# Moving Pool's power and ratio, the swap matmul and DVE's reciprocal within one round of an eight-batch language-model tower

## The reference

```python
h = tok(x)                                # embedding, causal 2-tap conv, relu
h = h + attn(layernorm(h), ...)           # linear recurrence, kept in logs, 4 heads x 64 states
#   x = exp(log_x - max over the 64 states + 2);  y = x @ C + u @ D
h = h + ffn(layernorm(h), ...)
#   normed -> x_attn = normed @ attn_w.T + attn_b + x
#   h1 = gelu(x_attn @ fc1.T + b1); y = h1 @ fc2.T + b2; out = gelu(y @ next_w.T + next_b)
```

## Time and profile before

| what | us |
|---|---|
| median of 3 runs | 189.66 (189.43 to 189.98) |
| the profiled execution, its own time | 189.79 |
| its span in the trace | 188.0 |
| PE busy, share of the span | 168.9, 90% |
| PE weight loads | 153.9, 82% |
| DVE busy | 136.7, 73% |
| POOL busy | 111.0, 59% |
| ACT busy | 107.4, 57% |

### The profile page before, as it was taken

One profiled execution on the slowest core, in us unless ns is written; L12 is line 12 of the kernel. 1 busy time (PEld: TensorE's weight loads), 2 busy tenths in 40 slices (PEclk: granted clock), 3 DMA queues, 4 the chain that ended last, 5 costly groups with the idle time before them and its releaser, 6 DMA issues.

```text
span 188.0 us, 3890 instructions
## 1 busy us (share of the span) xinstructions
PE 168.9 (90%) x1327; PEld 153.9 (82%) x1327; DVE 136.7 (73%) x409; ACT 107.4 (57%) x285; POOL 111.0 (59%) x178
## 2 busy tenths in 40 slices
PE   0497899999999998899898899999999999988972
PEld 0196779999999997787687799999998999987961
DVE  1859975765534546658988999998888896647993
ACT  3027997645543235434455484967949596775661
POOL 3106764799800000324979596696978969697761
PEclk9999999999999999999999999999999999999999
DMA  5994000000000000000000000000010100101103
GB/s 144 335 432 171 5 0 5 2 0 0 3 0 0 3 0 0 2 3 0 0 0 3 0 2 0 3 24 33 0 59 0 59 0 20 39 3 58 56 0 112
DMA packets 2327, 7.42 MB, mean 39 GB/s; under 512 B 254, under 2 KB 892, under 8 KB 2052
## 3 DMA queue, kind: packets, MB, share of 16 engines
q1 hardware_dynamic: 2162, 7.05, 10.0%
q10 hardware_dynamic: 146, 0.13, 0.3%
HBM read 5.09 MB, written 2.10 MB: 38 GB/s over the span
## 4 chain that ended last, share of the span: by engine, by line
PE 63%; POOL 10%; DVE 8%; ACT 8%; issue 7%; DMA 2%; POOLq 1%; ACTq 0%; DVEq 0%
PE bank L1072 8%; PE bank L934 8%; PE bank L1021 7%; PE bank L937 7%; PE bank L1092 6%; PE bank L962 5%; PE bank L1018 4%; PE bank L911 3%; PE bank L1041 3%; POOL hid_p L420 3%; PE bank L867 2%; PE bank L888 2%; ACT gel L543 2%; PE bank L951 2%; ACT hid_p L585 2%
## 5 line engine op out<-in xcount | busy, mean ns | idle before, releaser
L420 POOL TENSOR_TENSOR hid_p<-hid_f,hid_p 128x256 fp32r<-128x256 f32 x56 | 40.5, 745 | 16.7 <-ACT hid_p L585 12.5
L583 ACT ACTIVATE hid_f<-bank,pa 128x256 f32<-128x256 f32 x64 | 30.8, 485 | 13.4 <-PE bank L1072 12.7
L1072 PE MATMUL bank<-xaT_p,fc_p 128*128 128x256 f32 x192 | 35.0, 294 | 1.9 <-ACT corr L560 0.7
L1092 PE MATMUL bank<-hid_p,out_hi 128*128 128x256 f32 x128 | 32.2, 287 | 1.4 <-DVE hid_p L736 0.8
L492 ACT ACTIVATE X<-bank 128x128 f32<-128x128 f32 x64 | 17.6, 278 | 22.7 <-PE bank L937 22.5
L1072 PEld LDWEIGHTS bank<-xaT_p,fc_p 128*128 128x128 f32 x192 | 26.5, 189 | 4.7 <-issue 1.9
L1092 PEld LDWEIGHTS bank<-hid_p,out_hi 128*128 128x128 f32 x128 | 23.3, 188 | 2.5 <-POOL hid_p L420 1.4
L934 PE MATMUL bank<-uT,pa 128*128 128x128 f32 x128 | 25.2, 281 | 0.1
L585 ACT ACTIVATE hid_p<-bank,pa 128x256 fp32r<-128x256 f32 x48 | 23.5, 490 | 0.0
L937 PE MATMUL bank<-X,pa 128*128 128x128 f32 x120 | 23.2, 275 | 0.0
L427 POOL TENSOR_TENSOR E<-E,corr 128x248 f32<-128x248 f32 (+4 forms) x5 | 3.1, 625 | 32.0 <-ACT corr L568 32.0
(11 more groups left out here) (124 smaller groups left out, 369.9 us busy)
## 6 DMA issues: line engine op xcount, KB each, us to landing
fc_w<-in_fc SPq DMA_DIRECT2D x2, 2048.0 KB, 12.5
out<-res SPq DMA_DIRECT2D x7, 256.0 KB, 2.0
pb<-in_pack_b SPq DMA_DIRECT2D x1, 320.0 KB, 3.7
pa<-in_pack_a SPq DMA_DIRECT2D x1, 279.0 KB, 3.0
out<-res SPq DMA_DIRECT2D x2, 128.0 KB, 1.7
pc<-in_pack_c ACTq DMA_DIRECT2D x1, 128.5 KB, 2.9
pw<-in_pack_a SPq DMA_DIRECT2D x1, 64.0 KB, 3.4
emb_w<-in_emb SPq DMA_DIRECT2D x1, 62.5 KB
```

The costliest lines, as they stand in the source:

```text
L420: nc.gpsimd.tensor_tensor(hid_p[1][:, half, c, :], hid_f[:, m % HID_SLOTS, :], hid_p[0][:, half, c, :].bitcast(F32), ALU.subtract).then_in ...
L583: full = nc.scalar.activation(hid_f[:, m % HID_SLOTS, :], src, ACT.Gelu, bias=bias)
L1072: last = mm(bank[5 + n % 2][:, 0:HALF], fc1_p[w][:, e * HID + c * P:e * HID + (c + 1) * P], xaT_p[m][:, b % 2, half, :], start=(k == 0), s ...
L1092: last = mm(out_bank(b, half)[:, half * HALF:(half + 1) * HALF], out_p[w][:, e, c * CH:(c + 1) * CH], hid_p[m][:, half, c, :], start=(c == ...
```

## The change

Three things move; no operation is added or removed. On POOL the power, shift and ratio of batch j + 2 go ahead of everything else of step n = 3, that is ahead of unit 3's low part and, in round -1, ahead of two scan adds. On PE the swap goes ahead of mixer quarter 3. On DVE peak and reciprocal of batch j + 3 go from behind the statistics to ahead of xa's low part; a semaphore of their own (rcp_ready) takes the place of the chained wait.

```diff
@@ POOL
                 for j in range(-3, NB):
                     for n in range(8):
+                        b = j + 2
+                        if n == 3 and 0 <= b < NB:
+
+                            pool.wait_ge(v2_ready, b + 1)
+                            nc.gpsimd.tensor_tensor(rstd2[:, b, :, :].rearrange("p s q -> p (s q)"),
+                                                    spread2[:, b % 2, :, :].rearrange("p s q -> p (s q)"), neg_half[:],
+                                                    ALU.pow).then_inc(rstd2_ready, 1)
...
+                            nc.gpsimd.tensor_tensor(part[:, 0, :], part[:, 1, :], r0, ALU.mult).then_inc(ratio2_ready, 1)
                         if 0 <= j < DVE_ROUND or (j >= DVE_ROUND and n % 2 == 0):
...
-                        b = j + 2
-                        if n == 3 and 0 <= b < NB:
...
@@ DVE
                     high_parts(j, range(0, 2))
+                    b = j + 3
+                    if b < NB:
+                        dve.wait_ge(amax_ready, b + 1)
+                        dve.wait_ge(swap_done, b + 1)
+                        nc.vector.tensor_tensor(peak[:], amax[:, b % 2], bank_sw.rearrange("p (a i) -> p a i", a=NP),
+                                                ALU.max).then_inc(peak_ready, 1)
+                        dve.wait_ge(peak_ready, b + 1)
+                        nc.vector.reciprocal(rcp[:], peak[:]).then_inc(rcp_ready, 1)
                     b = j + 1
...
-                        dve.wait_ge(amax_ready, b + 1)
-                        dve.wait_ge(swap_done, b + 1)
-                        nc.vector.tensor_tensor(peak[:], amax[:, b % 2], bank_sw.rearrange("p (a i) -> p a i", a=NP),
-                                                ALU.max).then_inc(peak_ready, 1)
-                        dve.wait_ge(peak_ready, b + 1)
-                        chained(nc.vector.reciprocal(rcp[:], peak[:]))
+                        dve.wait_ge(rcp_ready, b + 1)
@@ PE
                         mixer_out(mixed, 2)
-                        mixer_out(mixed, 3)
                     if scaled < NB:
                         swap_quadrants(scaled)
+                    if 0 <= mixed < NB:
+                        mixer_out(mixed, 3)
                     fill(j, 2)
```

More of the change, by code:

```diff
@@ L213, in build @@
         ks_copied, full_ready = sem("ks_copied"), sem("full_ready")
-        amax_ready, swap_done, peak_ready, xh_ready = (
-            sem("amax_ready"), sem("swap_done"), sem("peak_ready"), sem("xh_ready"))
+        amax_ready, swap_done, peak_ready, rcp_ready, xh_ready = (
+            sem("amax_ready"), sem("swap_done"), sem("peak_ready"), sem("rcp_ready"), sem("xh_ready"))
         y_done, h2_ready, st2_ready, mv2_ready = sem("y_done"), sem("h2_ready"), sem("st2_ready"), sem("mv2_ready")
@@ L413, in _ @@
                     for n in range(8):
+                        b = j + 2
[4 more added lines that the diff above has]
+                                                    ALU.pow).then_inc(rstd2_ready, 1)
+                            pool.wait_ge(rstd2_ready, b + 1)
+                            if b >= 2:
+                                pool.wait_ge(xa_ready, b - 1)
+                            r0, r1, part = rstd2[:, b, 0, :], rstd2[:, b, 1, :], ratio2[:, b % 2]
+                            nc.gpsimd.tensor_tensor(shift2[:, b % 2], mv2[:, b, :, 0], r0, ALU.mult)
+                            chained(nc.gpsimd.tensor_tensor(part[:, 1, :], spread2[:, b % 2, 1, :], r1, ALU.mult))
+                            nc.gpsimd.tensor_tensor(part[:, 0, :], part[:, 1, :], r0, ALU.mult).then_inc(ratio2_ready, 1)
                         if 0 <= j < DVE_ROUND or (j >= DVE_ROUND and n % 2 == 0):
```

## The result

The changed kernel takes 192.77 us (median of 4 runs, 191.71 to 194.02) against 189.55 us before, a ratio of 1.0166 with a 95% interval of 1.0135 to 1.0197: 1.7% slower. The forecast was 193.0 us, +1.8%. The way and the size are right, but the time is put together differently from the forecast's sum, as the runs of the changed kernel lie at two levels, near 191.7 and near 193.9, and one part of it was not in the sum at all. No run took 193: with two runs at each level the median is the middle between them.

A forecast was written before the change was run, and what follows sets the result against it. The prediction took PE's own queue to bound the settled rounds. Its terms 1.1 + 0.7 + 1.6 - 0.15 made 3.25 us on the profiled 189.79: 193.0 us (+1.8%), range 190.4 to 194.5.

The forecast's parts named there:

- PE sets the pace, the rounds can only get longer: Settled rounds: PE runs by its own queue, so an 11 us round can't shorten, only lengthen where a step comes late.
- v2_ready 0.80 us late: DVE: peak now waits for the swap, so xa's low part and all up to v2_ready come 0.80 us later; bounds 0.69, 0.95.
- Rounds 1 to 4, 1.6 us: Unit 3's low part on POOL late, PE's matmul stalls 0.57, 0.40 us a round; 1.6 us in all, bounds 1.2 to 2.2.
- The transposes of h cost nothing in these rounds: Rounds 1 to 4: PE waits 0.3 us for the later h add, but this replaces an existing stall before fc1; no cost.
- Rounds -2 and -1, 1.1 us: Scan adds 10 and 11 behind the ratio start PE's round 0 1.81 late, 0.71 absorbed; 1.1 us, bounds 0.5 to 1.3.
- round 0, 0.7: Round 0: PE's wait for h counts in full and unit 3's low part is late; 0.7 us, bounds 0.4 and 1.2.
- the 0.52 was given back: Round 0: DVE's L805, 0.69 us long behind POOL's low parts, returns to 0.17; without this round 0 would cost 1.2.
- The tail, 0.15 back: Round 5 and after: power starts 0.84 sooner, but POOL's queue gains only 0.14 us; bounds 0 and 0.84.
- the queue's 0.14: Tail: POOL's queue gains 0.84 - 0.70 = 0.14 us, power sooner but one low part more behind it.
- The sum: Whole kernel: 1.1 + 0.7 + 1.6 - 0.15 = 3.25 us on the profiled 189.79, so 193.0.
- Rival (b): Low part in time in rounds 1 to 4, only rounds -1 and 0 pay: 1.7 us more, 191.4; chance 12%.

The follow-up runs named there:

- POOL's part alone: Kernel before with only POOL's power and ratio moved ahead of unit 3's low part and scan adds 10 and 11: 189.55 us, ratio 0.9989.
- the PE and DVE parts alone: Changed kernel with POOL's old order restored, so only swap, peak and reciprocal move: 190.03 us, ratio 1.0005.
- power first in round 5 alone: Kernel before with POOL's power and ratio ahead of unit 3's low part in round 5 only: 189.21 us (ratio 0.9969), again 189.49 (0.9979).
- the kernel with that wait alone: Swap, peak and reciprocal moved, POOL's power ahead of scan adds in round -1 only: seven runs 190.28 to 190.57, five 192.28 to 192.46; ratio 1.0074.
- round -1 undone: Changed kernel with POOL's power behind scan adds 10 and 11 again in round -1: 191.53 us (ratio 1.009), again 191.33 to 191.96 (1.0104).
- power first in rounds 1 to 5: Kernel before with POOL's power first in rounds 1 to 5, swap, peak and reciprocal as before: 189.32 us, ratio 0.9975.

## Why the prediction was right, step by step

The forecast named the way, the places and the chain of waits rightly; that its number met the measured median is in part luck, as the last point shows.

- **PE sets the pace, the rounds can only get longer.** Right but for 0.2 us: the shortest rounds 1 to 4 of any variant take 43.80 us in all (POOL's part alone), where the kernel before has 43.99.
- **v2_ready 0.80 us late.** Too much. (By its own terms it is 0.83: the sum to 128.29 holds two gaps of 0.03, not three.) The swap's result reached DVE 0.41 us after the swap's start (128.66 to 129.07), not 0.45, and xa's low part started 0.27 behind the start of the reciprocal, which takes 0.35, and the h add 0.69 behind that, where it was 0.80 before. From the end of mixer quarter 2 on PE to the end of L813 it is 3.95 us (128.66 to 132.61) where it was 3.39 (127.24 to 130.63): 0.56.
- **Rounds 1 to 4, 1.6 us.** The mechanism is shown by the two halves of the change, each free by itself. The size was 1.20, my lower bound, since it hangs on the term above: 0.34 at the matmul instead of 0.57. The wait for the low part that I had put at about 0.5 us in each of rounds 0 to 4 shows as 0.52 in round 0 and as 0.2 in the others.
- **The transposes of h cost nothing in these rounds.** Right: with v2_ready and the h add as late as in the changed kernel, the PE and DVE parts alone leave the rounds as they were.
- **Rounds -2 and -1, 1.1 us; round 0, 0.7.** Measured 0.98 and 0.57. PE's wait for h in round 0 is 0.58, but that this counts in full is refuted: the PE and DVE parts alone have the same wait (0.57) and pay 0.07 in that round. What costs there is the low part of unit 3, late behind v2_ready (PE's 0.52 at 113.18). L805 is back at 0.17 us (L812 of the kernel after), so the 0.52 was given back. By the rule of the Trainium skill (SBUF — State Buffer, "Who interferes with whom") it would be; the trace agrees.
- **The tail, 0.15 back.** It was 0.41. Counted from the transposes of xa in round 5, POOL begins its low parts 0.12 us sooner (169.41 and 171.63), which is the queue's 0.14, and the first two of them take 1.53 us instead of 1.93. Both together put PE's matmul of unit 7 (171.40 before, 173.21 after) 0.53 sooner, of which 0.41 is left at the end. The shorter low parts are a meeting of DVE and POOL that I had not looked at. Before, DVE's casts began at 169.39, 0.02 us ahead of POOL's low part, and the low part took 1.05 us; the timelines of both, and behind them those of the kernel after:

```profile
169.39 0.48 DVE L736 CAST hid_p<-hid_f 128x256 fp32r<-128x256 f32 x2
...
169.41 1.05 POOL L420 TENSOR_TENSOR hid_p<-hid_f,hid_p 128x256 fp32r<-128x256 f32 x1
```
```profile
170.90 1.67 DVE L735 CAST hid_p<-hid_f 128x256 fp32r<-128x256 f32 x2
...
170.39 1.28 POOL L457 TENSOR_TENSOR res<-gel,hT 128x512 f32<-128x512 f32 x1
171.63 0.78 POOL L435 TENSOR_TENSOR hid_p<-hid_f,hid_p 128x256 fp32r<-128x256 f32 x1
```

  After, xa is done sooner, the casts start while POOL is still at the addition of L457, and it is they that take 1.67 instead of 0.48, while POOL's first low part takes 0.78. The trace with the power first in round 5 alone has the same 1.67. That the first to start keeps the other waiting is read from these traces, not tested by a run of its own. The Trainium skill (SBUF — State Buffer, "Who interferes with whom") says so of the ports that DVE in its two-port mode and POOL share; these rows agree.
- **The sum.** 2.34 us at full clock, where I had 3.25: 192.1 would have been the right forecast for the lower level (189.79 + 2.34). The measured median is 193.0 because in more than half of the runs the clock falls behind the wait in round -1, 2.0 us that no step of mine held. The number was right by luck, by errors that cancel: three terms too large by 0.65 together and the tail's gift too small by 0.26, against one effect missed. I had written PE's start of round 0 as 1.81 late and had counted it only as time lost, not as time in which PE stands still.

Rival (b), a low part in time in rounds 1 to 4, came nearer to the sum at full clock (1.7 for 2.34, where I had 3.25), but its mechanism is refuted by PE's wait at 135.78 and by the 1.20 us that these rounds cost. Open are the 0.35 us by which the two levels differ beyond what the clock explains in the trace, and the meeting of DVE and POOL in the tail, which no run isolates.

## What to carry to other kernels

Before an instruction is moved ahead of another on an in-order engine, compare when its input comes with when the one passed over is wanted; here two moves that are free one by one cost 1.2 us together, as one made the input late and the other put the queue behind it. Move a step ahead only in the rounds where the critical engine waits for it: one round held all of the gain (0.4 to 0.6 us of the median, 0.3 in the traces). And count a new wait of TensorE twice, as time lost and as standing still that can lower its clock for the work behind it.

## What the runs showed of the hardware

- PE stood still 2.15 us, and in 6 of 11 runs of the changed kernel (5 of 12 of the kernel with that wait alone) the granted clock behind it was at 1.2 instead of 2.4 GHz for about 3.4 us, which cost 1.6 us on PE; the runs with it took 2.0 us longer. With 1.77 us in the same place it happened in none of 12 runs, with 0.68 us in none of 57 (the PE and DVE parts alone, round -1 undone, power first in round 5, power first in rounds 1 to 5). Eighteen matmul instructions with no use in the wait kept it away in five of five.
- A cast on DVE took 0.28 us alone and 0.93 us when it began at 170.90 while POOL was at work on an addition (L457); the other way round POOL's low part took 1.05 us instead of 0.74.
- One fp32 matmul of 128 columns shows as two instructions of about 0.11 us: nine of them are the 18 instructions that took 2.17 us.
